# Two pauses a step moved on GpSimd's queue, and ten semaphore increments taken out of TensorE's, in a graph attention kernel

## The chip, the cores and the metric

The kernel runs on one core of one Trainium2 chip. The time is that of the device, in microseconds, of one execution, as the median over several. Engines are named as in the profile: PE is TensorE's matrix products, PEld its weight loads, DVE is VectorE, ACT is ScalarE, POOL is GpSimd, SP is SyncE. Each has a queue of its own and runs its instructions in order; semaphores alone order one engine against another.

## The reference, cut to what matters

One layer of graph attention with a residual and a layer norm: 6250 nodes with 128 values each, 106250 edges, 8 heads of 16. The edges come ordered by destination, and attention is grouped by source.

```python
q = (x @ q_w.T + q_b).reshape(n, HEADS, HEAD_DIM)     # k, v the same way
row, col = (edge_index[0], edge_index[1])
scores = jnp.einsum('ehd,ehd->eh', q[row], k[col]) / jnp.sqrt(jnp.float32(HEAD_DIM))
scores = scores + edge_emb @ eb_w.T + eb_b
seg_max = jax.ops.segment_max(scores, row, num_segments=n)
exp_scores = jnp.exp(scores - seg_max[row])
seg_sum = jax.ops.segment_sum(exp_scores, row, num_segments=n)
attn = exp_scores / (seg_sum[row] + 1e-10)
out = jax.ops.segment_sum(attn[..., None] * v[col], row, num_segments=n)
out = out.reshape(n, HIDDEN) @ out_w.T + out_b
return _layernorm(x + out)
```

## The kernel before

**Stages.** After constants and a clearing of buffers (up to about 100 us) a stage called rank sorts the edges by source: it counts, finds for each edge its slot, and scatters a record of it (eight bias scores and indices) into DRAM. It also projects x to q, k and v. Then the stage attend takes the sorted records, gathers k and v of each edge, and sums. A merge of segments cut by tile borders, the output projection and the layer norm end the kernel.

**Steps.** Both stages go in steps of G = 8 tiles of 128 edges: 104 steps in rank, 110 in attend. Each engine has a function that issues its part of step s = 4k + v; the middle steps run in a hardware loop of four steps a pass, so the code of a step stands four times in it, and the first and last steps are laid out singly. Nothing plans the order: each queue holds what its step functions issue, in the order of the code, and waits by semaphores.

**Rank.** PE does, per step (line 720 on): count_up (656 to 668; a running count over the tiles, raises next_ready at its last product, line 662), same (line 674), turn_edges for the next step (645), biases (678 to 690), slots of the step before (692 to 706; three products per tile at lines 701, 702 and 703, then a transposition of the biases at line 706, which raises slots_ready), and in even steps a transposition of x (713), in odd ones the projection (717, 718), which waits for ACT's copy of x (line 782). ACT copies the counts (797), keeps the turned edges (775) and the biases (801), builds one-hots (758 to 767). DVE masks (822), and after slots_ready picks the slots and builds the row numbers (840 to 863, raises rows_ready). POOL scatters the 8 tiles' records with eight indirect transfers (line 624).

**The pauses of rank.** Ahead of the eight scatters of step s POOL waits until the rows of step s are there. Ahead of the fifth (t = 4) it waits for slots_ready at s + 2, that is, for the slot products of the step after (slots_ready counts one per step from 1). No data need this wait: it only holds POOL back.

**Attend.** PE does, per step: q_rows (24 products at line 1116), spread_rows (line 1102), turn_scores (lines 1131 and 1133; raises turned), sums (16 passes of fp32 at line 1151, in three banks), spread_rows, turn_keys (lines 1169 to 1174; raises keys_turned). DVE multiplies q by k (1311), reduces (1316), finds segment maxima, weighs v (1340; raises weighted) and adds sums to the accumulator (1302). ACT copies keys (1211), builds one-hots (1219, 1228, 1236), copies pieces (1260). POOL gathers k and v for 8 tiles with eight indirect transfers (line 1087).

**The pauses of attend.** Ahead of the eight gathers POOL waits for the buffer (weighted at s − 3) and for its records (rec_in). Ahead of the fifth it waits for turned at s − 1, again a wait that no data need.

**The increments.** `sem_inc(c["carrier"], 1)` raises a semaphore that nobody waits for.
## Time and profile before

| | |
|---|---|
| median of 3 runs | 3136.17 us |
| lowest and highest | 3133.39 and 3141.1 us |
| the profiled execution | 3146.63 us, its span 3144.9 us |
| busy of the span: PE, PEld | 1899.1 us (60%), 1498.0 us (48%) |
| busy of the span: DVE, ACT, POOL | 1604.0 us (51%), 1587.6 us (50%), 1758.0 us (56%) |
| line 1087, gathers | 880 times, 848.6 us busy, 616.0 us idle before them |
| line 624, scatters | 832 times, 817.5 us busy, 612.3 us idle before them |
| indirect transfers' queue | 70528 packets, 133.75 MB |

The page of the profile is one execution. "Idle before" is how long the engine had nothing running ahead of an instruction, with what ended it: a local engine's line, a DMA, "remote" where the profile names none, and "issue" where the engine waited for nothing that the profile shows. In a timeline, each row has the start and the duration in us.

### The profile page before, as it was taken

How to read it: one execution, taken by the hardware profiler on the slowest of the kernel's cores; microseconds unless marked ns; L12 is line 12 of the kernel's file. 1: busy time of each engine (PE TensorE's matmuls, PEld its weight loads, DVE VectorE, ACT ScalarE, POOL GpSimd, SP SyncE). 2: the span in 40 equal slices, each digit the busy share in tenths (PEclk: the TensorE clock that was granted, in tenths of full speed). 3: DMA queues.
4: the chain of work that ended last, by engine and by line, in shares of the span. 5: the costliest groups of instructions: out<-in, count | busy, mean ns of one | idle time of the engine just before them, and what ended most of it. 6: DMA issues, size and time to landing. Idle time of an engine off the chain costs nothing. (4 is left out here: it accounts for less than half of the span.)

```text
span 3144.9 us, 58004 instructions
## 1 busy us (share of the span) xinstructions
PE 1899.1 (60%) x14721; PEld 1498.0 (48%) x14722; DVE 1604.0 (51%) x4853; ACT 1587.6 (50%) x3672; POOL 1758.0 (56%) x1783
## 2 busy tenths in 40 slices
PE   8755666655556666556265666666665565665654
PEld 8644444444444444444154454554544444554543
DVE  9433333333333333333155666666565666666675
ACT  9555555555555555555044454444454444454433
POOL 6355555555555555555645556556555555555515
PEclk9877777777777777777566666766676676667666
DMA  4222222222222222221123333333333333323323
GB/s 157 80 73 73 72 72 64 70 70 64 71 72 72 72 69 65 72 64 53 53 73 88 84 82 87 83 85 85 82 86 83 84 85 85 83 83 87 82 64 95
DMA packets 161607, 245.59 MB, mean 78 GB/s; under 512 B 44647, under 2 KB 105003, under 8 KB 161289
## 3 DMA queue, kind: packets, MB, share of 16 engines
q0 software_dynamic: 70528, 133.75, 15.9%
q1 hardware_dynamic: 83914, 107.72, 11.9%
q10 hardware_dynamic: 7111, 3.47, 0.4%
q8 instruction: 26, 0.43, 0.1%
q14 instruction: 28, 0.23, 0.0%
HBM read 216.09 MB, written 28.70 MB: 78 GB/s over the span
## 5 line engine op out<-in xcount | busy, mean ns | idle before, releaser
L1087 POOL DMA_INDIRECT attend_kv<-kv_rows,attend_rec x880 | 848.6, 964 | 616.0 <-issue 266.6
L624 POOL DMA_INDIRECT sorted_records<-rank_record,rank_row x832 | 817.5, 983 | 612.3 <-PE rank_slot_ps L706 350.7
L1151 PE MATMUL attend_sum_ps<-attend_wv,attend_hot 128*128 128x136 f32 x1760 | 364.4, 382 | 171.1 <-ACT attend_piece L1260 97.2
L1151 PEld LDWEIGHTS attend_sum_ps<-attend_wv,attend_hot 128*128 128x128 f32 x1760 | 333.3, 279 | 204.1 <-issue 201.3
L1116 PE MATMUL attend_q_ps<-q,attend_hot_t 128*128 x2640 | 312.3, 246 | 168.1 <-issue 162.9
L822 DVE TENSOR_TENSOR rank_before<-rank_same_ps,below 128x512 bf16<-128x512 f32 x208 | 139.4, 689 | 399.9 <-PE rank_same_ps L674 287.5
L1116 PEld LDWEIGHTS attend_q_ps<-q,attend_hot_t 128*128 128x128 bf16 x2640 | 222.0, 106 | 241.5 <-issue 201.6
L1219 ACT ACTIVATE attend_off<-attend_lo_ps,attend_neg_row 128x512 bf16<-128x512 f32 x220 | 150.2, 683 | 327.5 <-remote 272.0
L758 ACT ACTIVATE rank_off<-iota_r,neg_lo 128x128 bf16<-128x128 bf16 x800 | 245.3, 391 | 0.0
L1302 DVE TENSOR_TENSOR acc<-attend_sum_ps,acc 128x136 f32 x880 | 221.5, 296 | 43.2 <-remote 31.5
L840 DVE COPY rank_record<-meta 128x24 int32 (+1 forms) x104 | 18.5, 178 | 428.6 <-PE rank_slot_ps L706 399.3
L1236 ACT CAST attend_hot<-attend_hot_b 128x1024 f32<-128x1024 bf16 x110 | 225.2, 2047 | 21.4 <-DVE attend_hot_b L1368 14.5
L1102 PE MATMUL attend_lo_ps<-identb,attend_row_b 128*128 128x128 bf16 x880 | 118.6, 265 | 193.0 <-issue 113.0
L1346 DVE TENSOR_TENSOR attend_reset<-attend_key_t 64x127 f32<-64x127 f32 x110 | 31.1, 283 | 387.1 <-ACT attend_key_t L1211 304.0
L717 PE MATMUL rank_project_ps<-w_kvq,rank_x_t 128*128 128x256 f32 x100 | 60.6, 709 | 268.2 <-ACT rank_x_t L782 268.2
L689 PE MATMUL rank_bias_ps<-rank_edges_t,w_eb 128*64 128x128 f32 x1664 | 206.0, 277 | 3.4 <-issue 3.4
L1311 DVE TENSOR_TENSOR attend_prod<-attend_q_ps,attend_kv 128x512 f32<-128x512 f32 x220 | 142.5, 684 | 111.9 <-remote 79.1
L689 PEld LDWEIGHTS rank_bias_ps<-rank_edges_t,w_eb 128*64 128x64 f32 x1664 | 179.9, 137 | 22.1 <-issue 22.1
L775 ACT COPY rank_edges_t<-rank_edge_ps 128x512 f32<-128x512 f32 x208 | 114.8, 587 | 144.2 <-PE rank_edge_ps L645 105.6
L801 ACT COPY rank_bias_t<-rank_bias_ps 64x128 f32<-64x128 f32 x104 | 27.1, 261 | 310.7 <-remote 288.6
L1102 PEld LDWEIGHTS attend_lo_ps<-identb,attend_row_b 128*128 128x128 bf16 x880 | 77.5, 118 | 213.8 <-issue 169.7
L1211 ACT COPY attend_key_t<-attend_key_ps 64x128 f32<-64x128 f32 x110 | 28.0, 255 | 269.3 <-remote 264.8
(293 smaller groups left out, 4391.8 us busy)
## 6 DMA issues: line engine op xcount, KB each, us to landing
rank_edges<-in_edge_attr SPq DMA_DIRECT2D x103, 512.0 KB
rank_lo_rows<-lo_by_tile SPq DMA_DIRECT2D x104, 256.0 KB
attend_kv<-kv_rows,attend_rec POOLq DMA_INDIRECT x880
sorted_records<-rank_record,rank_row POOLq DMA_INDIRECT x832
sorted_records<-prepare_blank POOLq DMA_DIRECT2D x8, 888.0 KB, 12.0
attend_rec<-sorted_records SPq DMA_DIRECT2D x110, 64.0 KB
merge_rows<-prepare_zero POOLq DMA_DIRECT2D x2, 1800.0 KB, 24.0
kv_rows<-rank_kv_out SPq DMA_DIRECT2D x49, 64.0 KB
```

Source lines behind the costliest of these rows:

```text
L624: pool.indirect_dma_start(rec_dram[:, :], bass.IndirectOffsetOnAxis(ap=row[:, v, t:t + 1], axis=0), record[:, v, t, :], None).then_inc(sca ...
L689: mm = pe.matmul(o, c["w_eb"][:, t, :], edges_t[:, u, t, :], start=False, stop=(t == G - 1))
L758: ins = act.activation(off2[:, t, :], c["iota_r"][:], ACT.Square, bias=r["neg_lo"][:, ds(s * G + t, 1)])
L822: dve.tensor_tensor(before[:, u, 4 * q:4 * q + 4, :], same_ps[:, q], bcast(c["below"][:], 1, 4), ALU.mult).then_inc(before_ready, 1)
L1087: pool.indirect_dma_start(kv[:, v, t, :], None, kv_dram[:, :], bass.IndirectOffsetOnAxis(ap=rec[:, v, t, H + 2:H + 3], axis=0)).then_inc(k ...
L1102: mm = pe.matmul(lo_ps[:, t, :], row_b[:, v, 4 * q + t:4 * q + t + 1].broadcast_to([P, P]), c["identb"][:], start=True, stop=True)
L1116: mm = pe.matmul(q_ps[:, q, t, :], hot_t[:, u, 4 * q + t, :], q3[:, ds(bucket[4 * q + t], 1), part, :], start=(part == 0), stop=(part == 2))
L1151: mm = pe.matmul(sum_ps[:, bank, i * W:(i + 1) * W], hot[:, u, t, :], wv[:, v % 4, t, :], start=True, stop=True)
L1219: act.activation(off2[:, q], lo_ps[:], ACT.Square, bias=neg_row[:, 0:1]).then_inc(squared, 1)
L1236: act.copy(hot[:, u], hot_b[:].rearrange("p n t -> p t n")).then_inc(hot_ready, 1)
L1302: dve.tensor_tensor(a, sum_ps[:, b, i * W:(i + 1) * W], a, ALU.add).then_inc(summed, 1)
L1311: dve.tensor_tensor(prod[:, q], q_ps[:, q], kv[:, v, 4 * q:4 * q + 4, 0:D], ALU.mult).then_inc(prod_ready, 1)
```

## The change

Rank on POOL: the wait for slots_ready at s + 2 goes from ahead of the fifth scatter to ahead of the sixth, and one for next_ready at s + 3 (the counting of step s + 2) is added ahead of the second. Attend on POOL: the pause ahead of the fifth gather is for keys_turned at s, and the one for turned at s − 1 goes ahead of the first. Both of these are raised in the same step of PE, two before. PE: ten increments go. Waits then stand at the products behind them, as far as one instruction can carry them; turn_scores and turn_keys keep one increment each, ahead of their products, for the waits that are left. In turn_keys the small products at lines 1171 and 1172 come ahead of the transposition of line 1169, and the wait on keys_kept becomes the last of three.

```diff
--- before.py
+++ after.py
@@ -618,7 +618,10 @@
             pool.wait_ge(meta_kept, s + 1)
             pool.sem_inc(c["carrier"], 1)
             for t in range(G):
-                if t == G // 2 and not until(k, v, 4) and inside(k, v, 2):
+                if t == 1 and not until(k, v, 4) and inside(k, v, 3):
+                    pool.wait_ge(next_ready, s + 3)
+                    pool.sem_inc(c["carrier"], 1)
+                if t == 5 and not until(k, v, 4) and inside(k, v, 2):
                     pool.wait_ge(slots_ready, s + 2)
                     pool.sem_inc(c["carrier"], 1)
                 pool.indirect_dma_start(rec_dram[:, :], bass.IndirectOffsetOnAxis(ap=row[:, v, t:t + 1], axis=0),
@@ -679,10 +682,8 @@
 
             s, u = 4 * k + v, v % 2
             pe.wait_ge(edges_kept, 2 * s + 2)
-            pe.sem_inc(c["carrier"], 1)
             if not until(k, v, 1):
                 pe.wait_ge(bias_t_kept, s)
-                pe.sem_inc(c["carrier"], 1)
             o = bias_ps[0:GH, 0:P]
             pe.matmul(o, c["b_eb"][:], c["ones"][0:1, :], start=True, stop=False)
             for t in range(G):
@@ -1081,8 +1082,11 @@
             pool.wait_ge(rec_in[v], 16 * (k + 1))
             pool.sem_inc(c["carrier"], 1)
             for t in range(G):
-                if t == G // 2 and not until(k, v, 4):
+                if t == 0 and not until(k, v, 8):
                     pool.wait_ge(turned, s - 1)
+                    pool.sem_inc(c["carrier"], 1)
+                if t == 4 and not until(k, v, 8):
+                    pool.wait_ge(keys_turned, s)
                     pool.sem_inc(c["carrier"], 1)
                 pool.indirect_dma_start(kv[:, v, t, :], None, kv_dram[:, :],
                                         bass.IndirectOffsetOnAxis(ap=rec[:, v, t, H + 2:H + 3], axis=0)
@@ -1123,10 +1127,9 @@
             own, ago = inside(k, v), inside(*off(k, v, -1))
             if own:
                 pe.wait_ge(score_ready, s + 1)
-                pe.sem_inc(c["carrier"], 1)
             if ago:
                 pe.wait_ge(max_ready, s)
-                pe.sem_inc(c["carrier"], 1)
+            pe.sem_inc(c["carrier"], 1)
             if own:
                 mm = pe.transpose(seg_ps[0:GH, 0:P], score[:, v].rearrange("p t h -> p (t h)"), c["ident"][:])
             if ago:
@@ -1137,16 +1140,12 @@
 
             s, u = 4 * k + v, v % 2
             pe.wait_ge(hot_ready, s + 1)
-            pe.sem_inc(c["carrier"], 1)
             pe.wait_ge(weighted, s + 1)
-            pe.sem_inc(c["carrier"], 1)
             for bank in range(NB):
                 if not until(k, v, 1):
                     pe.wait_ge(piece_kept, NB * (s - 1) + bank + 1)
-                    pe.sem_inc(c["carrier"], 1)
                 elif bank == NB - 1:
                     pe.wait_ge(weighted, s + 2)
-                    pe.sem_inc(c["carrier"], 1)
                 for i, t in enumerate(banks[bank]):
                     mm = pe.matmul(sum_ps[:, bank, i * W:(i + 1) * W], hot[:, u, t, :], wv[:, v % 4, t, :],
                                    start=True, stop=True)
@@ -1158,18 +1157,16 @@
             more, own, ago = inside(*off(k, v, 1)), inside(k, v), inside(*off(k, v, -1))
             if more:
                 pe.wait_ge(keys_ready, s + 2)
-                pe.sem_inc(c["carrier"], 1)
+            if ago:
+                pe.wait_ge(carried_ready, s)
             if own:
                 pe.wait_ge(keys_kept, s + 1)
-                pe.sem_inc(c["carrier"], 1)
-            if ago:
-                pe.wait_ge(carried_ready, s)
-                pe.sem_inc(c["carrier"], 1)
-            if more:
-                mm = pe.transpose(key_ps[0:GH, 0:P], keyf[:, (v + 1) % 4].rearrange("p t h -> p (t h)"), c["ident"][:])
+            pe.sem_inc(c["carrier"], 1)
             if own:
                 pe.matmul(key_ps[0:GH, P:P + 1], c["shift"][:], key_t[:, v, P - 1:P], start=True, stop=False)
                 mm = pe.matmul(key_ps[0:GH, P:P + 1], c["wrap"][:], key_t[:, (v - 1) % 4, P - 1:P], start=False, stop=True)
+            if more:
+                mm = pe.transpose(key_ps[0:GH, 0:P], keyf[:, (v + 1) % 4].rearrange("p t h -> p (t h)"), c["ident"][:])
             if ago:
                 mm = pe.transpose(key_ps[:, 192:192 + GH], carried[:], c["ident"][0:GH, 0:GH])
             mm.then_inc(keys_turned, 1)
```

## Rows read from the trace of the kernel before

**Rows 1.** Both stages: busy us of PE, PEld, DVE, ACT, POOL; PEclk, DMA, GB/s.

```profile
100.00:1480.00 1380.00, 830.04 (x7280) 637.68 (x7279) 518.80 (x1626) 740.78 (x1646) 783.49 (x799) 0.75 0.25 71
1560.00:3000.00 1440.00, 883.60 (x6035) 702.35 (x6035) 891.56 (x2679) 689.00 (x1607) 830.83 (x862) 0.68 0.32 84
```

**Rows 2.** Lines 706, 1133, whole span: xcount, ns min/median/max, first to last start.

```profile
L706 PEld LDWEIGHTS rank_slot_ps<-ident,rank_bias_t x104: 134/153/180, 120.5 to 1509.1; 64*128 64x128 f32 x104
...
L1133 PEld LDWEIGHTS attend_seg_ps<-ident,attend_seg_max x110: 134/178/180, 1588.9 to 3009.2; 64*128 64x128 f32 x110
```

**Rows 3.** POOL by line, both stages: count, busy us, mean ns, idle before it.

```profile
L624 POOL DMA_INDIRECT sorted_records<-rank_record,rank_row x796 | 782.8, 983 | 594.4 <-PE rank_slot_ps L706 345.4 <-issue 215.0 <-DVE rank_row L863 34.1
...
L1087 POOL DMA_INDIRECT attend_kv<-kv_rows,attend_rec x862 | 831.4, 965 | 606.8 <-issue 261.4 <-DVE attend_wv L1340 145.8 <-PE attend_seg_ps L1133 102.1
```

**Rows 4.** POOL's timeline, one run of eight: start, length, instruction, idle before.

```profile
815.27 0.96 POOL L624 DMA_INDIRECT sorted_records<-rank_record,rank_row  x1 [4.16 <-PE rank_slot_ps L706]
...
824.28 0.96 POOL L624 DMA_INDIRECT sorted_records<-rank_record,rank_row  x1 [0.30 <-issue]
```

**Rows 5.** Timeline of PE's weight loads, 820 to 828.

```profile
820.14 0.10 PEld L703 LDWEIGHTS rank_slot_ps<-rank_hot_hi,rank_before 128*128 128x128 bf16 x1
821.02 0.10 PEld L701 LDWEIGHTS rank_slot_ps<-rank_next_a,rank_hot_lo_t 128*128 128x128 bf16 x1 [0.79 <-issue]
...
826.88 0.10 PEld L702 LDWEIGHTS rank_slot_ps<-rank_next_r,rank_hot_lo_t 128*128 128x128 bf16 x1 [1.31 <-issue]
...
827.21 0.18 PEld L706 LDWEIGHTS rank_slot_ps<-ident,rank_bias_t 64*128 64x128 f32 x1
```

**Rows 6.** Weight loads by line, 100 to 1480.

```profile
L702 PEld LDWEIGHTS rank_slot_ps<-rank_next_r,rank_hot_lo_t 128*128 128x128 bf16 x807 | 68.4, 98 | 110.7 <-issue 110.7
...
L717 PEld LDWEIGHTS rank_project_ps<-w_kvq,rank_x_t 128*128 128x128 f32 x100 | 24.8, 308 | 278.3 <-ACT rank_x_t L782 278.2
L687 PEld LDWEIGHTS rank_bias_ps<-ones,b_eb 1*64 1x64 f32 x204 | 19.0, 130 | 17.9 <-issue 17.9
```

**Rows 7.** Timeline of weight loads, 799 to 817: where slots and counting end.

```profile
799.85 0.18 PEld L706 LDWEIGHTS rank_slot_ps<-ident,rank_bias_t 64*128 64x128 f32 x1
...
809.24 0.83 PEld L674 LDWEIGHTS rank_same_ps<-rank_hot_lo_t 128*128 128x128 bf16 x8
...
814.18 0.13 PEld L706 LDWEIGHTS rank_slot_ps<-ident,rank_bias_t 64*128 64x128 f32 x1
...
816.17 0.46 PEld L674 LDWEIGHTS rank_same_ps<-rank_hot_lo_t 128*128 128x128 bf16 x8
```

**Rows 8.** Timeline of ACT, 805 to 828.

```profile
805.20 0.25 ACT L782 COPY rank_x_t<-rank_project_ps 128x128 f32<-128x128 f32 x1
...
827.02 0.26 ACT L801 COPY rank_bias_t<-rank_bias_ps 64x128 f32<-64x128 f32 x1 [4.68 <-remote]
```

**Rows 9.** Weight loads by line, 1560 to 3000.

```profile
L1151 PEld LDWEIGHTS attend_sum_ps<-attend_wv,attend_hot 128*128 128x128 f32 x1694 | 319.7, 278 | 194.9 <-issue 192.0
```

**Rows 10.** POOL's timeline, first and last gather of a run of twelve.

```profile
2123.90 0.95 POOL L1087 DMA_INDIRECT attend_kv<-kv_rows,attend_rec  x1 [3.24 <-DVE attend_wv L1340]
...
2138.06 0.95 POOL L1087 DMA_INDIRECT attend_kv<-kv_rows,attend_rec  x1 [0.31 <-issue]
```

**Rows 11.** Timeline of weight loads, 2124 to 2168.

```profile
2124.20 0.18 PEld L1133 LDWEIGHTS attend_seg_ps<-ident,attend_seg_max 64*128 64x128 f32 x1 [0.28 <-issue]
...
2141.78 0.18 PEld L1133 LDWEIGHTS attend_seg_ps<-ident,attend_seg_max 64*128 64x128 f32 x1 [0.26 <-issue]
...
2146.27 0.13 PEld L1174 LDWEIGHTS attend_key_ps<-ident,attend_carried 64*128 64x128 f32 x1
...
2150.25 0.14 PEld L1133 LDWEIGHTS attend_seg_ps<-ident,attend_seg_max 64*128 64x128 f32 x1
...
2155.46 0.14 PEld L1174 LDWEIGHTS attend_key_ps<-ident,attend_carried 64*128 64x128 f32 x1
...
2167.48 0.50 PEld L1151 LDWEIGHTS attend_sum_ps<-attend_wv,attend_hot 128*128 128x128 f32 x2 [3.48 <-issue]
```

## The prediction

> **What bounds the kernel now.** I read the stages side by side first [rows 1]. Counting and scattering (about 100 to 1510 us) and attention (about 1560 to 3030) carry nearly all of the time, and no engine is busy in more than 62% of either: DVE's 891.56 of 1440 us in attention is the most, POOL has 783.49 of 1380 and 830.83 of 1440. So it is a loop of waits, and the length of a step is the figure to follow. Line 706 (end of slots) runs 104 times from 120.5 to 1509.1: (1509.1 − 120.5)/103 = 13.48 us a step. Line 1133 runs 110 times from 1588.9 to 3009.2: 13.03 us a step [rows 2]. Together 104 × 13.48 + 110 × 13.03 = 2835 of 3145 us.
>
> Next, POOL by line: its indirect transfers take 0.98 and 0.96 us each, and most of its idle time is for PE's line 706 in ranking (345.4 us) and for DVE's weighing and PE's line 1133 in attention (145.8 and 102.1) [rows 3]. A gather starts 1.29 us after the one before it: (824.28 − 815.27)/7 in ranking [rows 4], (2138.06 − 2123.90)/11 in attention [rows 10]. Eight of them are 10.3 us, below both steps: POOL alone isn't the bound.
>
> Then what POOL's wait hides. PE's own idle time before the slot products has no releaser ("issue"): 110.7 us before line 702 alone in ranking [rows 6], 192.0 us before line 1151 in attention [rows 9]. The timelines place it. A run of eight scatters goes from 815.27 to 825.24 [rows 4]. PE's slot products follow each other in hundredths of a microsecond until 820.14; then each starts some 0.7 us after the last, and the twelve that are left take until 827.21, 7.1 us [rows 5], where line 706 at 814.18, ahead of that run, came 4.9 us after counting's end at 809.24, everything included [rows 7]. ACT's line 801 starts only at 827.02 with 4.68 us of idle time whose releaser isn't a local engine [rows 8], though the product that it copies is issued ahead of all slot products. In attention, a run of twelve gathers (2123.90 to 2139.0 [rows 10]) lies in a distance of 17.6 us between two line 1133s, 2124.20 and 2141.78; the next distance, over a run of four, is 8.5 us [rows 11]. **My reading:** after some five transfers without a break (5 to 6 us) the other engines get their instructions thinly, until 1 to 2 us after the run ends. A pause that splits runs is then worth more than the time POOL loses in it.
>
> The Trainium skill speaks against this reading (Runtime: NRT & Kernel Launch, section Instruction fetch mechanics): the sequencer fetches ahead by its own queue, so fetching is "mostly hidden", apart from taken branches. The trace's gaps of 0.79 and 1.31 us before single products in a straight stretch [rows 5] differ from it, whatever their cause; by the page, the pauses would buy nothing and the time would stay at 3136.
>
> **Ranking, part by part.** Let S be the end of slots (line 706) and C the end of counting (the line 674 behind it). A pair of steps runs S 799.85, C 809.24, S 814.18, C 816.17, S 827.21: gaps of 9.4, 4.9, 2.0 and 11.0, sum 27.4 us [rows 5, 7]. The 9.4 is the odd step's projection, which waits for ACT's x_t (278.2 us over the stage [rows 6]; the copy is at 805.20 [rows 8]). The 11.0 is the same work as the 4.9 with a thin window on it: 6.1 us of loss a pair. Now one pause (t = 4) on S: all eight scatters of two half steps go in one run behind each S. After: one pause at t = 5 on S and one at t = 1 on C two steps ahead, so runs of four, X behind S and Y behind C, each 4 × 1.29 = 5.2 us, each released 1.1 us after its event's product starts (815.27 against 814.18 [rows 4, 7]), 0.8 us after that product ends.
> - Behind the short gap (S 814.18, C 816.17) X is still going when C comes, so Y joins it: the same run of eight at the same place, hence the same 11.0. Behind the long gap (9.4), X and Y are apart. But that Y starts 1 us after C and lasts until 6.2, while the next S is at 4.9: the next X joins on, and its Y too: twelve without a break, thin from about the next C on.
> - What is gained if this joining comes apart: at most the thin window less the pauses. 6.1 less some 2 us of POOL's waits = 4 us a pair, 23.4. What is lost if twelve run on: the window is longer by half a run of four, about 2.7 us, 30.1. Three pairs of ten good and seven bad would be 28.1 us. I take this value, +0.7 a pair, since the short gap of 2.0 is in the trace of every pair; × 52 pairs = **+36 us**, with bounds −208 and +140.
> - Queued behind the new wait at t = 1 are seven scatters of the step and the wait of the next; their record buffers are reused four steps on, and nobody waits for scatters sooner. So the wait itself costs nobody, unless POOL becomes late: 16 × 1.29 = 20.6 a pair is 6.8 below 27.4.
> - Biases drops two increments. Line 687's idle time of 17.9 us over its 102 pairs of loads [rows 6] is 0.18 us for both. It lies beside the wait for ACT and DVE in the long gap and is partly on the path in the short one; bounds 0 and 0.18 × 104 = 19 us. I take nothing for it, inside the range.
>
> **Attention, part by part.** Now POOL pauses at t = 0 on the weighing and at t = 4 on line 1133 (turned); where both are there, runs grow to twelve. After: t = 0 on turned (line 1133) and t = 4 on keys_turned (line 1174), both of the same step of PE. The wait on weighing stays and is then long met.
> - Between line 1133 and line 1174 lie 2141.78 to 2146.27, 4.5 us, and 2150.25 to 2155.46, 5.2 us [rows 11]. The first run A needs 5.2. So the second, B, comes either straight behind A (a run of eight, thin in its last 4 us) or with a small break. No run of twelve is left, and none is sure to be four.
> - Joined: 0.8 (release, as above) + 8 × 1.29 + 1.7 (until instructions flow again: 826.88 against the run's end at 825.24 [rows 4, 5]) + 0.5 (lines 1131 and 1133 behind it, an estimate) = 13.3, hardly other than 13.03. Apart: 4.5 to 5.2 for the first half and 4.0 for the second (2146.27 to 2150.25) is 8.5 unhindered, so that POOL's 10.3 plus two releases of 0.8 = 11.9 is the floor, 11.4 where one release is covered.
> - Eight of the ten increments lie here. PE's sequencer stands at each. Unhindered they are 0.09 us (half of 0.18 [rows 6]), 0.7 us a step beside other waits. In a thin window they cost what any instruction costs: 3.48 us ahead of the first sums product at 2167.48 [rows 11], where five of them stand in a row, 0.7 each; four of the five go. That was so in the steps with a long run, 42 of 110 by count of the gathers' runs. Bounds 0 and 42 × 2.8 = 118 us; part of it is the same time as in the line above, so I don't add it.
> - turn_keys issues its two small products ahead of the transposition of keyf; they now wait for key_t at their own queue place, and the transposition behind them. The distance is 0.5 us, and next's ACT copy (line 1211) waits for the last of them in any case: nothing.
> I take the middle of 13.03 and 11.4, since the two distances read lie one on each side of about 5: 12.2, less 0.85 × 110 = **−94 us**; bounds −180 and +60 (13.6 a step, when B is late and every run is eight).
>
> **Sum.** The profiled execution took 3146.6 us, 10.5 above the median of 3136.2. 3146.6 + 36 − 94 = 3088.6; against the median **3078 us**.
>
> **The rivals.**
> - *Both loops split as meant.* Rank 23.4 a pair: −208; attention 12.0 a step: −112. 3136 − 320 = 2816. For it: the pauses sit exactly between halves. Against it: the short gap of 2.0 and B straight behind A.
> - *Runs join to twelve in ranking (slower).* Y behind the long gap's C runs into X and the next Y; +2.7 × 52 = +140, and attention at 13.6, +60: 3336. It decides wherever S follows C by less than 6.2 us, as at 814.18; it fails if DVE's placing, thin too, holds the next X back and so makes a break of its own.
> - *Nothing moves.* The thin stretches aren't caused by unbroken runs but by something that comes along with them; the pauses then only move POOL's waits, which already cover 43% of its time (594.4 of 1380 [rows 3]): within 10 us of 3136. The page of the skill named above would give this case too.
>
> **How the numbers follow.** Chances: forecast 0.36 (about 3000 to 3150), both split 0.20 (2780 to 2900), joined 0.32 (3180 to 3400), nothing moves 0.12. Range 2860 to 3320: it leaves out half of the second case and a quarter of the third. A measurement of this kernel tells 0.3%, some 9 us, from no change. Faster: 0.32 + 0.20 = 0.52; same 0.12 + 0.01 = 0.13; slower 0.32 + 0.03 = 0.35. Most of the cases lie on both sides, so the likeliest one's own range is 3000 to 3150.
>
> **What would show it.** In the changed kernel's POOL timeline: the lengths of runs (4, 8 or 12). In ranking, idle time at line 624 released by line 662, and the issue idle time of lines 701 to 703: gone if split, up if joined. S to S for a pair: 23.4, 27.4 or 30. In attention, line 1133's distances even out, without 17.6s; line 1151's 192 us of issue falls by more than half. I would be wrong if runs of four show and PE still starts thinly, or if the step doesn't follow the run lengths.

## The result and the profile after

The changed kernel took 3155.93 us (median of 8 runs, 3150.35 to 3160.6), the kernel before 3141.27 us (8 runs, 3133.39 to 3146.8) on the same chip: ratio 1.0053, with a 95% interval of 1.0038 to 1.0069. It is slower by half a percent. The two stages moved in opposite ways. First the line that ends the slots (706 before, 707 after) and the one that raises turned (1133 before, 1136 after): count, duration in ns, first and last start; to be held against [rows 2].

```profile
L707 PEld LDWEIGHTS rank_slot_ps<-ident,rank_bias_t x104: 134/136/179, 120.7 to 1556.4; 64*128 64x128 f32 x104
...
L1136 PEld LDWEIGHTS attend_seg_ps<-ident,attend_seg_max x110: 134/179/180, 1640.4 to 3018.9; 64*128 64x128 f32 x110
```

Ranking's last slots come at 1556.4 in place of 1509.1, 47.3 us later: (1556.4 − 120.7)/51.5 = 27.9 us a pair of steps, against 27.0. Attention goes from 13.03 to (3018.9 − 1640.4)/109 = 12.65 us a step, 41.8 us less. Between the stages and behind them 5 us more went.

Ranking's weight loads by line, stretch 100 to 1480 (count, busy us, mean ns, idle before), against [rows 6]:

```profile
L704 PEld LDWEIGHTS rank_slot_ps<-rank_hot_hi,rank_before 128*128 128x128 bf16 x776 | 64.7, 97 | 80.1 <-issue 79.6
L703 PEld LDWEIGHTS rank_slot_ps<-rank_next_r,rank_hot_lo_t 128*128 128x128 bf16 x776 | 64.5, 97 | 64.1 <-issue 63.9
L702 PEld LDWEIGHTS rank_slot_ps<-rank_next_a,rank_hot_lo_t 128*128 128x128 bf16 x776 | 63.0, 96 | 87.2 <-issue 86.0 <-DVE rank_before L823 0.9
...
L718 PEld LDWEIGHTS rank_project_ps<-w_kvq,rank_x_t 128*128 128x128 f32 x96 | 23.8, 308 | 304.9 <-ACT rank_x_t L783 300.4 <-issue 4.5
```

And POOL by line, the same stretch, against [rows 3]:

```profile
L627 POOL DMA_INDIRECT sorted_records<-rank_record,rank_row x765 | 754.3, 986 | 621.3 <-issue 234.9 <-PE rank_slot_ps L707 140.5 <-PE rank_next_ps L665 125.5
```

Lines 702 to 704 are lines 701 to 703 of before: 229.5 us of issue idle time in all, in place of 307.5 (112.6, 110.7 and 84.2). So the gaps between slot products did get fewer, but the wait for ACT's x_t has grown from 278.2 to 300.4 (line 718, was 717). POOL is now released partly by line 665 (counting), as the new pause has it. POOL's timeline (start, duration; idle before) shows the runs in one pair and the start of the next:

```profile
797.83 0.96 POOL L627 DMA_INDIRECT sorted_records<-rank_record,rank_row  x1 [2.72 <-PE rank_slot_ps L707]
...
801.87 0.96 POOL L627 DMA_INDIRECT sorted_records<-rank_record,rank_row  x1 [0.30 <-issue]
807.39 0.96 POOL L627 DMA_INDIRECT sorted_records<-rank_record,rank_row  x1 [4.55 <-PE rank_next_ps L665]
...
811.18 0.96 POOL L627 DMA_INDIRECT sorted_records<-rank_record,rank_row  x1 [0.30 <-issue]
814.34 0.96 POOL L627 DMA_INDIRECT sorted_records<-rank_record,rank_row  x1 [2.20 <-PE rank_slot_ps L707]
...
823.33 0.96 POOL L627 DMA_INDIRECT sorted_records<-rank_record,rank_row  x1 [0.31 <-issue]
827.53 0.96 POOL L627 DMA_INDIRECT sorted_records<-rank_record,rank_row  x1 [3.24 <-PE rank_slot_ps L707]
```

Four scatters from 797.83, four from 807.39, then eight from 814.34 to 824.29, behind the short gap. Over ranking, 75 of 133 runs are of four and 56 of eight; before, 99 of 100 were of eight. The trace also keeps the moment at which an engine raises a semaphore, in records that the views above don't print. POOL starts 0.80 us behind the raise of slots_ready in both kernels (814.34 behind 813.54; before, 815.27 behind 814.47). Line 707's weight load stands at 812.50 here, but its product only at 813.23, so measured from the weight load the start is 1.8 us and no longer the 1.1 of [rows 4, 7].

Attention's weight loads by line, stretch 1640 to 3000, against [rows 9]:

```profile
L1150 PEld LDWEIGHTS attend_sum_ps<-attend_wv,attend_hot 128*128 128x128 f32 x1680 | 363.3, 315 | 69.1 <-issue 54.8 <-ACT attend_piece L1257 12.3
L1120 PEld LDWEIGHTS attend_q_ps<-q,attend_hot_t 128*128 128x128 bf16 x2545 | 249.0, 106 | 379.8 <-issue 332.2
```

The second of these lines in the kernel before, stretch 1560 to 3000:

```profile
L1116 PEld LDWEIGHTS attend_q_ps<-q,attend_hot_t 128*128 128x128 bf16 x2616 | 219.5, 106 | 240.3 <-issue 201.0
```

POOL in the changed kernel, 1640 to 3000, against [rows 3]:

```profile
L1091 POOL DMA_INDIRECT attend_kv<-kv_rows,attend_rec x843 | 805.4, 955 | 566.6 <-remote 263.5 <-issue 216.1 <-DVE attend_wv L1337 40.1
```

The sums (line 1150, was 1151) lost 137 us of issue idle time (192.0 to 54.8), and q_rows (line 1120, was 1116) gained 131 (201.0 to 332.2): it moved. POOL's releaser is mostly one that the profile doesn't name. The timelines of one step, POOL's first:

```profile
2403.92 0.95 POOL L1091 DMA_INDIRECT attend_kv<-kv_rows,attend_rec  x1 [3.06 <-remote]
...
2412.73 0.95 POOL L1091 DMA_INDIRECT attend_kv<-kv_rows,attend_rec  x1 [0.30 <-issue]
2416.72 0.95 POOL L1091 DMA_INDIRECT attend_kv<-kv_rows,attend_rec  x1 [3.04 <-remote]
```

PE's weight loads in the same stretch:

```profile
2405.10 0.18 PEld L1136 LDWEIGHTS attend_seg_ps<-ident,attend_seg_max 64*128 64x128 f32 x1 [0.28 <-issue]
...
2411.02 0.18 PEld L1171 LDWEIGHTS attend_key_ps<-ident,attend_carried 64*128 64x128 f32 x1 [0.23 <-issue]
...
2414.15 0.10 PEld L1120 LDWEIGHTS attend_q_ps<-q,attend_hot_t 128*128 128x128 bf16 x1 [1.26 <-issue]
2415.58 1.21 PEld L1120 LDWEIGHTS attend_q_ps<-q,attend_hot_t 128*128 128x128 bf16 x11 [1.33 <-issue]
```

And ACT:

```profile
2415.81 0.26 ACT L1240 ACTIVATE attend_wv<-attend_score 128x64 f32<-128x64 f32 x1 [6.37 <-remote]
```

Eight gathers from 2403.92 to 2413.68, then 3.04 us of nothing, then eight more: 12.8 us. Turned (line 1136) comes at 2405.10, 1.2 us into the run, so the pause on it is met when POOL gets there, four gathers on. The product that raises keys_turned (line 1171) starts at 2411.02 and ends at 2411.39, 2.3 us before the run ends; yet POOL's next run starts at 2416.72, and PE loads weights only once between 2412.9 and 2415.58.

The records of the raises settle what POOL waits for. keys_turned is raised at 2415.92, 4.5 us after the end of its product and 2.2 us after the last gather. POOL's instruction that reads it ends 0.04 us later, and the gather starts 0.80 us behind the raise, as in ranking. ACT's 6.37 us are such a wait too: it needs DVE's scores, raised at 2413.47, and PE's sums, whose last product ended at 2409.79 and whose last raise comes at 2415.79, and it starts at 2415.81. DVE works on from 2410.59 to 2414.90. So POOL and ACT read their semaphores at once. What is late is PE: its raises and, within a long run, its next products.

That holds over the stage. Of keys_turned's raises, 105 can be told between 1640 and 3000: 98 come over 1 us after the end of their product, the middle one 4.8 us, and half of those 98 come 2.2 us or more after POOL's last gather. POOL's next gather follows 0.80 us behind the raise. The raises of DVE and ACT come about 0.01 us after the end of the instruction. The view of waits prints such a late raise of PE as "remote", since no engine has just finished what raises it:

```profile
POOL attend_kv L1091 <- remote: 263.5, 91, 3.1
```

This is the largest of POOL's waits in attention, with the total in us, the times and the longest.

### The profile page after: what moved, and what is told of

It is laid out like the page before. It is cut to its first block and busy times, and to the rows that moved or that the text cites. A ratio compares the mean times of both kernels' runs of the same rounds, so it can differ in the third digit from the quotient of the medians.

```text
span 3155.6 us, 57485 instructions
## 1 busy us (share of the span) xinstructions
PE 2030.9 (64%) x14721; PEld 1603.1 (51%) x14722; DVE 1604.4 (51%) x4853; ACT 1566.3 (50%) x3672; POOL 1751.5 (56%) x1783
## 5 line engine op out<-in xcount | busy, mean ns | idle before, releaser
L1091 POOL DMA_INDIRECT attend_kv<-kv_rows,attend_rec x880 | 840.5, 955 | 581.6 <-remote 263.5
L1120 PE MATMUL attend_q_ps<-q,attend_hot_t 128*128 x2640 | 361.4, 269 | 297.7 <-issue 224.1
L1120 PEld LDWEIGHTS attend_q_ps<-q,attend_hot_t 128*128 128x128 bf16 x2640 | 259.0, 106 | 393.9 <-issue 344.2
L1150 PE MATMUL attend_sum_ps<-attend_wv,attend_hot 128*128 128x136 f32 x1760 | 410.2, 420 | 60.2 <-issue 40.3
L1150 PEld LDWEIGHTS attend_sum_ps<-attend_wv,attend_hot 128*128 128x128 f32 x1760 | 378.9, 314 | 79.5 <-issue 55.9
L1240 ACT ACTIVATE attend_wv<-attend_score 128x64 f32<-128x64 f32 x110 | 28.2, 256 | 598.9 <-remote 490.0
L690 PE MATMUL rank_bias_ps<-rank_edges_t,w_eb 128*64 128x128 f32 x1664 | 212.9, 282 | 5.9 <-issue 5.7
L718 PEld LDWEIGHTS rank_project_ps<-w_kvq,rank_x_t 128*128 128x128 f32 x100 | 24.8, 308 | 320.2 <-ACT rank_x_t L783 315.6
L665 PE MATMUL rank_next_ps<-rank_hot_hi,rank_hot_lo 128*128 128x416 bf16 (+3 forms) x832 | 149.1, 338 | 11.3 <-issue 11.0
L798 ACT CAST rank_next_a<-rank_next_ps 128x468 bf16<-128x468 f32 x104 | 56.0, 539 | 198.8 <-PE rank_next_ps L665 175.7
```

The lines of the kernel that those rows point to most:

```text
L665: mm = pe.matmul(table[:, t + 1:, :], hot_lo[:, u, t, :], bcast(hot_hi[:, v, t, :], 1, G - t), start=False, stop=(t == G - 1))
L690: mm = pe.matmul(o, c["w_eb"][:, t, :], edges_t[:, u, t, :], start=False, stop=(t == G - 1))
L1091: pool.indirect_dma_start(kv[:, v, t, :], None, kv_dram[:, :], bass.IndirectOffsetOnAxis(ap=rec[:, v, t, H + 2:H + 3], axis=0)).then_inc(k ...
L1120: mm = pe.matmul(q_ps[:, q, t, :], hot_t[:, u, 4 * q + t, :], q3[:, ds(bucket[4 * q + t], 1), part, :], start=(part == 0), stop=(part == 2))
L1150: mm = pe.matmul(sum_ps[:, bank, i * W:(i + 1) * W], hot[:, u, t, :], wv[:, v % 4, t, :], start=True, stop=True)
```

## The experiments

Ten runs of the change or its parts and eight of other kernels. Two kinds of chip turned up, and no number here is clear without that: on chips 0, 1 and 7 and in the first comparison the kernel before takes 3122 to 3141 us, on chips 2, 6 and 13 it takes 2456 to 2458 us. Each ratio is against the kernel before on the same chip. "A pair" is twice the mean distance of the slots' last line, from its first and last start. No trace was kept of the kernel before on any of these chips but the first; where attention or ranking of before is needed there, it is read from a kernel that leaves that stage unchanged.

**The parts of the change.** One part each, the rest as before:

```diff
 a_rank_pauses, a2_rank_pauses: only
-                if t == G // 2 and not until(k, v, 4) and inside(k, v, 2):
+                if t == 1 and not until(k, v, 4) and inside(k, v, 3):
+                    pool.wait_ge(next_ready, s + 3)
+                    pool.sem_inc(c["carrier"], 1)
+                if t == 5 and not until(k, v, 4) and inside(k, v, 2):
                     pool.wait_ge(slots_ready, s + 2)
 b_attend_pauses: only
-                if t == G // 2 and not until(k, v, 4):
+                if t == 0 and not until(k, v, 8):
                     pool.wait_ge(turned, s - 1)
                     pool.sem_inc(c["carrier"], 1)
+                if t == 4 and not until(k, v, 8):
+                    pool.wait_ge(keys_turned, s)
+                    pool.sem_inc(c["carrier"], 1)
 c_pe_waits: only the ten increments and the order in turn_keys
 d_attend_and_pe: b and c together
```

> Only the two pauses of ranking are changed; attention and PE's waits are those of before. The trace of the changed kernel has its last slot product 47 us later than before (1556.4 against 1509.1) and attention 42 us shorter. Theory (the pauses decide, by how long POOL's transfers run unbroken): ranking loses all of these 47 us here too, 3141 + 47 = 3188, with a pair of steps at 28.4 us in place of 27.3. Rival (PE's waits decide, biases' standing at its products lets PE's sequencer run on into something worse): ranking stays at 27.3 us a pair, 3141.

> Only the two pauses of attention are changed. Theory: the step is one run of eight gathers and the break behind it, 12.7 us in place of 13.03, so 3141 - 42 = 3099, and POOL's runs are nearly all of eight. Rival (the eight increments taken from PE in attention made its gain): no gain from the pauses alone, 3141.

> Only PE is changed: ten increments out, waits at the products, the order in turn_keys; the pauses are those of before. Theory: increments cost only where instructions come thinly; 42 of 110 steps of attention had a long run, with at most 2.8 us each, mostly hidden behind POOL: 3141 less 0 to 40 us, about 3125; ranking at 27.3 us a pair. Rival (the increments made attention's gain): 3099.

> The whole change but the pauses of ranking. If the parts add up, ranking as before (27.3 us a pair) and attention as in the changed kernel (12.65 us a step): 3141 - 42 = 3099, faster than both kernels. If ranking's loss came from PE's biases, 3156 as with the whole change.

Chip 1, before 3122.24 us. a: 3141.08, ratio 1.0071 (1.0034 to 1.0108). b: 3098.87, 0.9924 (0.9906 to 0.9941). c: 3122.85, 0.9999 (0.9989 to 1.0010). d: 3098.13, 0.9916 (0.9897 to 0.9935). The line that raises turned, in b:

```profile
L1136 PEld LDWEIGHTS attend_seg_ps<-ident,attend_seg_max x110: 134/179/179, 1583.0 to 2961.1; 64*128 64x128 f32 x110
```

The same in d:

```profile
L1133 PEld LDWEIGHTS attend_seg_ps<-ident,attend_seg_max x110: 134/179/180, 1588.8 to 2963.2; 64*128 64x128 f32 x110
```

12.64 and 12.61 us a step, as in the whole change. The pauses alone make attention's gain; the increments and the order in turn_keys are worth nothing that can be measured, alone or beside the pauses. The gain is smaller than in the first comparison, 23 us: attention with its old pauses takes 12.86 and 12.87 us a step on this chip (a and c), against 13.03 in [rows 2]. The kernel d, the change without ranking's part, is 0.8% faster than the kernel before. For ranking, a shows the sign and 19 us of loss, less than the 47 expected; a pair was 27.0 us against 26.8 to 26.9 in b, c and d.

**Do the parts act on one another?** The whole change, and ranking's part whole (two pauses, and biases without increments):

> The whole change once more, beside its parts on one chip. The pauses of ranking alone cost 0.71% (0.34 to 1.08), those of attention gave 0.76% (0.59 to 0.94), PE's part 0.01%. If the parts add up: ratio 1.000 less or more 0.4. If the whole change is again 0.53% slower, something in it comes only of parts together: the pauses of ranking with the two increments less in biases.

> Ranking's part of the change whole (two pauses, and biases without increments), attention as before. Theory (parts act on one another in ranking: a pair of steps was 28.4 us in the whole change, 27.6 with the pauses alone): a pair of 28.4 us, about 1.1 x 52 = 57 us over the kernel before, ratio about 1.015. Rival (the difference was between one chip or run and another): a pair of 27.6, ratio 1.007.

Both fell on chip 2, before 2457.66 us: ratios 0.9998 (0.9988 to 1.0007) and 0.9996 (0.9986 to 1.0005). They answer another question. POOL there in the whole change (line 627, stretch 100 to 1140):

```profile
L627 POOL DMA_INDIRECT sorted_records<-rank_record,rank_row x794 | 773.5, 974 | 263.7 <-issue 227.5 <-DVE rank_row L864 22.0 <-PE rank_slot_ps L707 13.4
```

And its two loops, first and last start:

```profile
L707 PEld LDWEIGHTS rank_slot_ps<-ident,rank_bias_t x104: 133/135/137, 120.7 to 1149.2; 64*128 64x128 f32 x104
...
L1136 PEld LDWEIGHTS attend_seg_ps<-ident,attend_seg_max x110: 133/138/180, 1218.8 to 2316.7; 64*128 64x128 f32 x110
```

A pair is 20.0 us, about two steps of eight scatters at 1.26 us each; attention's step is 10.07 us, eight gathers at 1.25. POOL runs through all of ranking's 832 scatters without one gap over 0.6 us, the slots' line keeps it waiting 13.4 us in the whole stage, and there is no gap between PE's slot products. Here PE's raises are not late: all 110 of keys_turned come 0.01 us after the end of their product. POOL's wait for them, the counterpart of the 263.5 us above (stretch 1219 to 2316):

```profile
POOL attend_kv L1091 <- PE attend_key_ps L1171: 13.1, 43, 0.3
```

So the pauses are nearly always met and cost next to nothing. The kernel and its transfers are the same on both kinds of chip; what differs is how soon PE's semaphores are raised and how close its products follow.

On chip 0, before 3124.31 us, ranking's part again in both forms:

> Ranking's two pauses alone, once more, beside the next kernel on the same chip. Slow chip: 27.6 us a pair, ratio 1.007. Fast chip: 20.5 a pair, 1.000.

> Ranking's two pauses and biases without increments. Slow chip: if the increments matter beside these pauses, 28.4 us a pair, ratio 1.015; if the difference was between chips, the same as the kernel with the pauses alone, 1.007. Fast chip: 1.000.

a2: 3151.79 us, 1.0089 (1.0064 to 1.0113); e2: 3155.96, 1.0102 (1.0074 to 1.0129). A pair is (1527.3 − 121.3)/51.5 = 27.3 in a2 and 27.3 in e2, their last slots at 1527.3 and 1527.6. So the increments of biases make no difference that shows beside the pauses either. Ranking's loss is that of its pauses. Attention's part gave −0.76 (b) to −0.84% (d), ranking's +0.71 (a) to +1.02% (e2); the whole would stand at −0.13 to +0.26%, with 0.3 to 0.4 either way, and the whole was measured at +0.53 (0.38 to 0.69) in the first comparison. Two more tries fell on chips 6 and 13 (2456.32 and 2457.29 us):

> The whole change on a slow chip. If the parts add up: -0.76 + 0.89 = +0.1%, ratio 1.001 (0.998 to 1.004), ranking 27.7 us a pair, attention 12.65 a step. If they act on one another: 1.005 with ranking at 28.4. On the fast chip 1.000.

> The whole change on a slow chip. If the parts add up: -0.76 + 0.89 = +0.1%, ratio 1.001 (0.998 to 1.004), ranking 27.7 us a pair, attention 12.65 a step. If they act on one another: 1.005 with ranking at 28.4. On the chip of 2456 us 1.000.

Ratios 1.0000 (0.9991 to 1.0009) and 0.9997 (0.9988 to 1.0006). Whether the rest is the parts together or the first chip stays open; by the traces, both stages moved further on that chip (+47 and −42 us) than their parts did on chips 0 and 1.

**Is it the unbroken run?** The kernels i, i2, j, n, o, q and r change how long POOL's transfers run, and g their number.

> Left out: the scatters of tiles 4 to 7 of each step of ranking, so that their records stay blank; the pause on the slots stands in the middle of the four. Nothing else changes in what PE, ACT and DVE do. Theory (runs of eight make the other engines' instructions thin after 5 us): with runs of four the 11.0 us from counting to slots behind the short gap becomes about 5, a pair of steps 21 to 23 us, ranking 52 x 5 = 260 us shorter, and the issue idle time of the slot products' weight loads (110.7 us at line 702) falls to near nothing. Rival (it is not POOL's transfers that hold PE back): a pair stays at 27.3.

```diff
-            for t in range(G):
-                if t == G // 2 and not until(k, v, 4) and inside(k, v, 2):
+            for t in range(G // 2):
+                if t == 2 and not until(k, v, 4) and inside(k, v, 2):
```

It leaves out half of the scatters, so half of the records stay blank. It fell on chip 2, one run of 2440.69 us: a pair of 20.0 us, as with eight scatters. It can't speak on thin stretches, since there are none there. It shows that the loop of PE and ACT needs about 20 us a pair by itself, so that POOL's 20.3 and theirs are level.

> Ranking as before, but POOL clears a spare buffer of 2048 values ahead of scatters 1 and 5 of each step (about 2 us each by 0.52 us for 512), so that transfers never run unbroken for more than four. Work of POOL a step: 8 x 1.27 + 2 x 2.3 = 14.8 us. Theory (what matters is transfers without a break, whatever breaks them): PE's thin stretches vanish, the step is POOL's 14.8 in place of 13.65, a pair 29.6, +1.15 x 104 = +120 us, with line 702's issue idle time near nothing. Rival A (thin stretches come of POOL being busy, or of the number of transfers in a time of some 10 us): line 702's issue idle time stays at 100 us and more. Rival B: they vanish and POOL's work overlaps its transfers, a pair of 24 to 27.

> The kernel before without either pause: POOL scatters and gathers as soon as its rows or buffers are there. On the chip where the kernel before takes 2458 us nothing is thin and POOL runs without a break anyway: same time there, ratio 1.00. On a chip like the first two (3120 to 3140 us) the theory (unbroken transfers make every other engine's instructions thin) says that without pauses nothing ends a run until POOL's own data are late: runs longer than eight, more than half of the time thin, ranking above 27.3 us a pair, ratio 1.02 to 1.15. Rival (the pauses cost more than they give, POOL's 20.3 us a pair becomes the bound): faster than before, 0.85 to 0.98.

> The breaks of 1.8 us by a clearing ahead of scatters 1 and 5 once more. On the chip of 2458 us the step of ranking was POOL's own work, 26.8 us a pair, with no thin stretch to remove. On a slow chip the theory says the same 26.8 us a pair (against 27.3 with the pauses), since runs of four leave PE's instructions fluent and POOL's work is the only bound. Rival (thin stretches come of the number of transfers in a time or of POOL being busy): more than 30 us a pair, and slot products with issue idle time as before.

```diff
 i_breaks_2us, i2_breaks_2us (ranking; j_breaks_1us: 1024 in place of 2048)
+    idle = sb("idle", [P, 2, 2048], I32)
...
+                if t % (G // 2) == 0:
+                    if t == 0 and not until(k, v, 1):
+                        pool.wait_ge(cleared, 2 * s + 3)
+                        pool.sem_inc(c["carrier"], 1)
+                    pool.memset(idle[:, t // 4], 0).then_inc(cleared, 1)
                 pool.indirect_dma_start(rec_dram[:, :],
 n_no_pauses
-                if t == G // 2 and not until(k, v, 4) and inside(k, v, 2):
-                    pool.wait_ge(slots_ready, s + 2)
-                    pool.sem_inc(c["carrier"], 1)
...
-                if t == G // 2 and not until(k, v, 4):
-                    pool.wait_ge(turned, s - 1)
-                    pool.sem_inc(c["carrier"], 1)
```

i fell on chip 2, i2 and n on chip 7 (before 3127.11 us). i took 2804.01 us against 2457.66, i2 3134.9 against 3127.11, one run each. The line of the slots in i:

```profile
L713 PEld LDWEIGHTS rank_slot_ps<-ident,rank_bias_t x104: 134/137/180, 121.0 to 1472.3; 64*128 64x128 f32 x104
```

In i2:

```profile
L713 PEld LDWEIGHTS rank_slot_ps<-ident,rank_bias_t x104: 133/136/180, 121.1 to 1472.2; 64*128 64x128 f32 x104
```

POOL in i2 by line, stretch 100 to 1480:

```profile
L630 POOL DMA_INDIRECT sorted_records<-rank_record,rank_row x798 | 776.3, 973 | 215.3 <-issue 198.2 <-POOL rank_idle L629 16.4 <-DVE rank_record L848 0.8
L629 POOL MEMSET rank_idle<- 128x2048 int32 x200 | 364.5, 1822 | 21.7 <-DVE rank_row L870 21.6
```

Its slot products in the same stretch:

```profile
L710 PEld LDWEIGHTS rank_slot_ps<-rank_hot_hi,rank_before 128*128 128x128 bf16 x832 | 73.0, 101 | 0.0
L709 PEld LDWEIGHTS rank_slot_ps<-rank_next_r,rank_hot_lo_t 128*128 128x128 bf16 x832 | 72.8, 101 | 0.0
L708 PEld LDWEIGHTS rank_slot_ps<-rank_next_a,rank_hot_lo_t 128*128 128x128 bf16 x832 | 72.6, 101 | 187.0 <-issue 186.8 <-DVE rank_before L829 0.2
```

DVE's longest wait there (total us, times, longest):

```profile
DVE rank_record L847 <- DMA sorted_records<-rank_record,rank_row: 770.8, 92, 10.4
```

And the two loops of n:

```profile
L703 PEld LDWEIGHTS rank_slot_ps<-ident,rank_bias_t x104: 133/136/180, 120.2 to 1619.1; 64*128 64x128 f32 x104
...
L1127 PEld LDWEIGHTS attend_seg_ps<-ident,attend_seg_max x110: 133/178/221, 1703.0 to 3347.9; 64*128 64x128 f32 x110
```

With a clearing of 1.82 us after each four scatters, ranking takes the same on both kinds of chip: last slots at 1472.3 and 1472.2, the last scatter at 1535.3 in both. The gaps between slot products are gone in i2: nothing at lines 709 and 710, where 702 and 703 had 110.7 and 84.2 us before; the 186.8 us of line 708 lie ahead of the first product of a step, and i has them too on chip 2 (206.6). POOL works for more of the time than before and issues as many scatters, so the gaps come neither of its being busy nor of the number of transfers, but of transfers without a break.

Two limits go with that. First, i2 is no faster. POOL never stands still for more than 0.3 us in it, DVE waits for the scatters to land before it refills a record (770.8 us), and the loop is POOL's own work. The last scatter comes at 1535.3, against 1531.8 in the trace of the kernel before; the 26.2 us a pair of the slots' line only say how far ahead of POOL the slots are. Second, PE's raises are late even with runs of four: slots_ready's by 3.1 us in the middle in i2, 0.01 us in i. Hardly anything waits for them there.

Without any pause (n) all is worse: 3477.9 us, ratio 1.1129 (1.1054 to 1.1205), 29.1 us a pair and 15.1 a step of attention. 46 of attention's 60 runs are of sixteen, and slots_ready's raise comes 6.9 us late in the middle, against 0.01 us in the kernel before, while the issue idle time of the three lines of slot products is lower than before, 155.8 us against 307.5. By these figures the late raises weigh more than the gaps between products. The two pauses together, which look as if they only cost time, are worth 11% on chip 7.

> As the breaks of 2048 values, with half of them: POOL clears 1024 values (about 0.95 us) ahead of scatters 1 and 5, ranking only. POOL's work is 8 x 1.266 + 2 x 1.1 = 12.3 us a step. On a slow chip: if a break of 1.1 us suffices, a pair of 24.7 us against 27.3, 52 x 2.6 = 135 us faster, ratio 0.957. If a break must be near 2 us, the stretches of thin instructions come back from the second run on: a pair of 27 to 30 us, ratio 1.00 to 1.04. On the fast chip a pair of 24.7 against 20.5: 220 us slower, 1.09.

> The breaks of 1024 values in both loops, with ranking's pause on the slots kept and attention's pause taken out. If 1.1 us suffices: ranking 24.7 us a pair, attention 8 x 1.255 + 2 x 1.1 = 12.2 us a step against 13.0, together 135 + 88 = 223 us faster, ratio 0.93 on a slow chip. If it doesn't: attention above 13, ratio above 1.0. On the fast chip: 24.7 a pair and 12.2 a step, 220 + 235 us slower, 1.18.

```diff
 o_breaks_both: j_breaks_1us, and in attention
-                if t == G // 2 and not until(k, v, 4):
-                    pool.wait_ge(turned, s - 1)
-                    pool.sem_inc(c["carrier"], 1)
+                if t in (0, 4):
+                    pool.memset(idle[:, t // 4], 0).then_inc(c["idled"], 1)
```

(with a wait of each clearing for the one a step earlier). Attention's pause is out in o. Chip 0. Two of j's weight loads by line, stretch 100 to 1480:

```profile
L709 PEld LDWEIGHTS rank_slot_ps<-rank_next_r,rank_hot_lo_t 128*128 128x128 bf16 x832 | 66.9, 96 | 12.0 <-issue 11.8
...
L724 PEld LDWEIGHTS rank_project_ps<-w_kvq,rank_x_t 128*128 128x128 f32 x100 | 24.8, 309 | 352.1 <-ACT rank_x_t L789 186.6 <-issue 165.4
```

The line of its slots:

```profile
L713 PEld LDWEIGHTS rank_slot_ps<-ident,rank_bias_t x104: 134/135/179, 121.1 to 1433.0; 64*128 64x128 f32 x104
```

o's sums, stretch 1560 to 2980:

```profile
L1162 PEld LDWEIGHTS attend_sum_ps<-attend_wv,attend_hot 128*128 128x128 f32 x1624 | 322.6, 276 | 388.0 <-issue 384.0
```

And POOL in o, the same stretch:

```profile
L1098 POOL DMA_INDIRECT attend_kv<-kv_rows,attend_rec x808 | 772.1, 956 | 221.1 <-issue 212.7 <-DVE attend_wv L1351 0.3
L1097 POOL MEMSET attend_idle<- 128x1024 int32 x202 | 195.0, 965 | 233.7 <-DVE attend_wv L1351 230.0 <-issue 3.5
```

j: 3064.46 us, 0.9810 (0.9782 to 0.9837), 25.5 us a pair: faster than the kernel before, but short of the 24.7 that was worked out from POOL's own work. Issue idle time is back in part, 11.8 us at line 709 and 165.4 of the 352.1 at 724: a break of 1.1 us clears most of the gaps between slot products, not all. o: 3159.87, 1.0124 (1.0091 to 1.0157). Ranking is as in j, but attention goes from about 12.9 to 13.86 us a step with runs of four nearly throughout, 384.0 us of issue idle time ahead of the sums (192.0 in [rows 9]), and 230.0 us of POOL waiting for the weighing. So breaks of 1.1 us are worth less in attention than the pause that they replace, and more than nothing (15.1 in n, on another chip); why they do less there than in ranking wasn't tried.

> Ranking with the pause of before and the breaks of 1024 values (ratio 0.981 alone), attention's pauses and all of PE's waits as in the change (0.992 alone). The stages follow one another, so they add up: 0.973 on a slow chip, 26.0 us a pair and 12.65 a step. On the fast chip 24.8 a pair: 1.09.

> Ranking with one break of 1024 values a step, ahead of scatter 1 (the middle of the run of eight); the pause on the slots stays ahead of scatter 5. POOL's work is 10.1 + 1.1 = 11.2 us a step. Theory: the pause makes the break at scatter 5 as long as the slots come late, the clearing makes that at scatter 1; as soon as slots are early, scatters 5 to 8 join on and thinness returns, so it settles between the two: 24.5 to 26.5 us a pair, ratio 0.965 to 0.99. Rival (a break of 1.1 us does little, and in the kernel with two the second one did the work): 27.3 a pair or more, 1.00.

q is j's ranking with the change's attention; r has one clearing of 1024 values a step, ahead of scatter 1. Both fell on chip 6: 2618.23 us, 1.0658 (1.0642 to 1.0675), and 2536.21, 1.0328 (1.0312 to 1.0343). There each clearing only adds POOL's time: 22.8 and 21.3 us a pair against 20.0. That they would gain on the other kind of chip (0.973 for q, as the sum of 0.981 and 0.992) is argued, not shown. The same ranking that gains 1.9% in j on one kind of chip costs 6.6% in q on the other, where attention's part of the change is worth nothing (the whole change: 1.0000).

## Why the prediction was wrong

**The sign and the size.** Forecast 3078 us in 2860 to 3320, faster; measured 3155.93, slower by 0.53%. On the profiled executions the sum was +36 − 94 = −58 us; it came to +47 − 42, with 5 more between and behind the stages, +11 (3157.36 against 3146.63).

**The reading of the bound: the cost held, the cause did not.** Long runs without a break are dear: breaks take the gaps between slot products away (i2) or most of them (j), and without any pause the kernel is 11% slower (n). But I read that the other engines get their instructions thinly. The raises say otherwise. In the run of [rows 4], ACT's line 801 waits 4.68 us for the biases of PE, whose last product ended at 819.94 and whose raise came at 826.995; ACT started at 827.02. Of the stretches of over 1 us in which POOL's queue stood still in the changed kernel, 608 us in all, 581 end within 0.3 us of a raise that it waits for, 513 of them a raise of PE's. Thin are PE's own products, and late are its raises. The reading also lacked a condition: on chips 2, 6 and 13 neither is seen. The rule of the Trainium skill that I set against it (Runtime: NRT & Kernel Launch, section Instruction fetch mechanics, fetching "mostly hidden") isn't contradicted by any of this: nothing here shows that fetching is what is late, and the profile's two instruction queues carry 25 and 28 packets in the changed kernel on either kind of chip.

**Ranking: the size came out, by luck.** +36 us forecast, +47 measured, bounds −208 and +140. The +36 is the mean of a pair of 23.4 at three in ten and one of 30.1 at seven in ten, and neither came. The runs are four, four and eight; the twelve that I feared never came, since slots_ready is raised only after the four have ended (812.14, raise 813.54). Behind the short gap, where I wrote "the same 11.0", counting to slots fell from 10.9 to 9.4 us in the mean. The loss is in the three other distances of the pair, for which my sum had nothing but the 2.7 us of the runs of twelve: slots to counting 9.6 to 10.4 and 1.8 to 2.8, counting to slots behind the long gap 5.0 to 5.7. They grew by 2.6 us together. The raise of the biases fits: over 1 us late in 87% of the steps, 50% before.

**Attention: the step that failed.** "I take the middle of 13.03 and 11.4, since the two distances read lie one on each side of about 5: 12.2." The 4.5 and 5.2 us are distances from product to product, line 1133 to line 1174. POOL doesn't wait for products but for raises, and those were in the same trace: turned at 2142.16 and keys_turned at 2148.97, 6.8 us, and 2150.54 and 2166.70, 16.2 us. Both distances lie far above 5; keys_turned came 2.4 and 11.0 us after the ends of its products. The 0.8 us from the event to POOL was right. In the changed kernel the pauses hardly ever split a run: 86 of the 104 runs between 1640 and 3000 are of eight, the last four gathers of one step and the first four of the next, and the step is 12.65. I had computed the joined case too, at 13.3. It came out shorter, at 12.8 in the step shown: 9.8 us from the first gather to the end of the last, 2.2 until the raise, 0.8 until POOL starts. −94 should have been 110 × (12.65 − 13.03) = −42.

**The increments: right at nothing.** I left them out of the sum with bounds of 0 to 118 us in attention; c gives 0.9999 (0.9989 to 1.0010), all ten together. The 3.48 us ahead of the sums did fall (issue idle time 192.0 to 54.8 in the whole change), but the time turned up elsewhere: in c alone, ahead of the same line, as a wait for ACT as well. The sums of c by line (stretch 1560 to 2980):

```profile
L1144 PEld LDWEIGHTS attend_sum_ps<-attend_wv,attend_hot 128*128 128x128 f32 x1695 | 324.3, 277 | 284.2 <-ACT attend_piece L1251 141.6 <-issue 138.8
```

The issue idle time is 138.8 us, 53 less than in [rows 9], and 141.6 us of waiting for ACT's pieces stand in its place. So an increment less moved the wait from one instruction to another. For biases a2 and e2 agree within their intervals.

**The chances.** The slower rival, joined to twelve at 3336, had the right sign by the wrong mechanism and some twelve times the size (200 us, 6.4%). I had given "faster by over 0.3%" 0.52 although one term of +36 and one of −94 each hung on how often a run splits. With −42 in place of −94 my own sum is −6 us, no change; the 11 us that ranking cost beyond its term and the 5 outside the stages made it slower.

## What to carry to other kernels

Read a wait from the raise that ends it, and not from the product that makes it: here the two lay up to 11 us apart in the steps that the forecast used, and "remote" beside a wait, or idle time without a releaser, was the sign. Where GpSimd issues indirect transfers in a loop, look at the run lengths in its timeline first. On one kind of chip a clearing of 1.0 us after each four scatters made the kernel 1.9% faster, one of 1.8 us cleared all gaps between slot products but bought no time, since GpSimd itself became the bound, and no pause at all cost 11%. A pause on an event splits a run only where the event is raised after the run's end; one that is already met is no pause. And time such a change on more than one chip: what gained 2% on one kind cost more on the other.

## What the runs showed of the hardware

Two kinds of chip: the same kernel in 3122 to 3141 us and in 2456 to 2458 us, some 27% apart, while GpSimd's transfers start 1.25 to 1.27 us apart on both. On the slower kind, TensorE's products come some 0.7 us apart late in a long run [rows 5], and its semaphores are raised late: keys_turned 4.8 us after the product in the middle, 2.2 us after the last gather, in the changed kernel, and 0.01 us on chip 2. ScalarE and VectorE nearly always raise theirs within about 0.01 us on both kinds, and ScalarE and GpSimd go on within 0.02 to 0.04 us of the raise in the step shown.

What in the chip makes it, and why only on some, no run here shows. Three things go along with it and were not separated. The granted clock of TensorE is lower on the slower kind, 0.69 against 0.79 over the changed kernel; products are longer there (the sums' 0.42 us against 0.38), but by far less than the raises are late. The transfers' own packets take as long on both kinds, 0.12 us in the mean. And the traces of the slower kind lack many records of raises (of VectorE's weighing, 93 of 110 are there, on chip 2 all), so that a part of the recording itself in the delay isn't excluded.
